# Slot scatters without a bound, slot tiles loaded ahead of features, and squares ahead of products in layer one

## What is computed

```
h = relu(layernorm(x));  x = x + GCN(h)            # two graph convolutions 64 -> 128 -> 64
h = relu(layernorm(x));  x = x + KGAT(h)

def KGAT(h):
    h_proj = einsum('nd,rde->rne', h, relation_weight)      # 32 relations
    att = sum(h_proj[etype, src] * tanh(h_proj[etype, dst] + efeat), -1)
    a = softmax of att over the edges of one destination
    h_nb = segment_sum(h[src] * a, dst)
    return leaky((h + h_nb) @ w1.T) + leaky((h * h_nb) @ w2.T)
```

## Time and profile before

| what | us |
|---|---|
| median of 3 runs | 4033.5 |
| lowest and highest | 4032.55 and 4057.6 |
| the profiled execution, its own time | 4044.76 |
| its span in the profile | 4043.0 |
| busy: POOL / VectorE (DVE) / TensorE (PE) / ScalarE (ACT) | 2830.5 / 2549.4 / 1968.6 / 1865.5 |

### The profile page before, as it was taken

How to read it: one execution, slowest core, us unless ns; L and a number is a source line. 1 busy time by engine, 2 the same in 40 slices (tenths; PEclk the granted TensorE clock), 3 DMA queues, 4 the chain that set the end, 5 groups by cost and what they waited for, 6 DMA issues and landing times.

```text
span 4043.0 us, 42919 instructions
## 1 busy us (share of the span) xinstructions
PE 1968.6 (49%) x10767; PEld 1528.2 (38%) x10767; DVE 2549.4 (63%) x5153; ACT 1865.5 (46%) x5179; POOL 2830.5 (70%) x4049
## 2 busy tenths in 40 slices
PE   5719996576666322222100005524545475766663
PEld 2206664455545312222100004413434454665553
DVE  9957775777777489999732215754866456443442
ACT  0018884667667477778310013102212113887773
POOL 8888884888885488888577776666666400877787
PEclk9959997555555555555555557657656666666666
DMA  6667874444544366666422225325334331221220
GB/s 228 232 252 251 266 261 154 138 154 159 158 141 148 104 196 211 206 207 203 118 61 79 67 82 150 91 58 146 101 97 128 113 89 47 70 58 55 61 61 21
DMA packets 261704, 547.95 MB, mean 136 GB/s; under 512 B 107792, under 2 KB 119930, under 8 KB 261462
## 3 DMA queue, kind: packets, MB, share of 16 engines
q1 hardware_dynamic: 179702, 445.68, 33.0%
q0 software_dynamic: 81760, 99.52, 9.9%
HBM read 275.18 MB, written 273.83 MB: 136 GB/s over the span
## 4 chain that ended last, share of the span: by engine, by line
POOL 38%; issue 16%; ACT 11%; PE 10%; DVE 7%; DMA 3%; POOLq 0%; SPq 0%; DVEq 0%; ACTq 0%
POOL arena L1348 19%; POOL result L1343 9%; POOL slot_rows L1343 8%; ACT work L1519 3%; ACT work L1530 3%; PE banks L1879 2%; DMA work<-slot_rows 2%; PE banks L1846 2%; POOL pause L1356 2%; PE banks L1947 1%; ACT arena L1590 1%; PE banks L2027 1%; ACT work L1753 1%; PE banks L1871 1%; ACT work L1762 1%
## 5 line engine op out<-in xcount | busy, mean ns | idle before, releaser
L1343 POOL DMA_INDIRECT result<-work,outi x392 | 474.8, 1211 | 315.4 <-DVE work L1050 193.8
L1343 POOL DMA_INDIRECT slot_rows<-work,dsafe x392 | 396.5, 1011 | 282.1 <-POOL pause L1361 186.1
L1348 POOL DMA_INDIRECT work<-in_x,dsafe x392 | 439.1, 1120 | 112.6 <-POOL pause L1356 104.9
L1348 POOL DMA_INDIRECT arena<-g_by_node_and_edge,m_idx x392 | 433.5, 1106 | 116.1 <-POOL pause L1356 108.2
L1348 POOL DMA_INDIRECT arena<-h_by_node_and_edge,m_idx x392 | 406.0, 1036 | 111.5 <-POOL pause L1356 59.9
L1348 POOL DMA_INDIRECT arena<-input_and_place_by_node,src_i x252 | 302.6, 1201 | 74.9 <-POOL pause L1356 73.0
L1838 PE MATMUL banks<-ident,work 128*128 128x128 f32 x392 | 101.7, 411 | 462.5 <-ACT arena L1501 410.2
L1933 PE MATMUL banks<-ident,work 128*128 128x128 f32 x556 | 123.6, 366 | 388.5 <-DMA work<-slot_rows 277.4
L1530 ACT ACTIVATE work<-work,q_stat 128x64 f32<-128x64 f32 x784 | 264.7, 428 | 1.0 <-DVE q_stat L624 0.9
L1519 ACT ACTIVATE work<-work,q_stat 128x64 f32<-128x64 f32 x784 | 260.2, 338 | 0.0
L1838 PEld LDWEIGHTS banks<-ident,work 128*128 128x128 f32 x392 | 70.2, 217 | 484.9 <-issue 426.9
(11 more groups left out here) (338 smaller groups left out, 6910.3 us busy)
## 6 DMA issues: line engine op xcount, KB each, us to landing
slot_rows<-work SPq DMA_DIRECT2D x64, 834.0 KB
work<-slot_rows SPq DMA_DIRECT2D x139, 384.0 KB, 3.4
input_and_place_by_node<-arena SPq DMA_DIRECT2D x49, 528.0 KB, 3.0
g_by_node_and_edge<-arena SPq DMA_DIRECT2D x49, 512.0 KB
arena<-x_of_destination SPq DMA_DIRECT2D x56, 448.0 KB, 5.1
work<-g_by_node_and_edge SPq DMA_DIRECT2D x49, 512.0 KB, 3.7
h_by_node_and_edge<-work SPq DMA_DIRECT2D x49, 512.0 KB, 2.7
work<-h_by_node_and_edge SPq DMA_DIRECT2D x56, 448.0 KB, 4.0
```

What stands on the lines that cost most here:

```text
L1343: pool.indirect_dma_start(out=table[:, :], out_offset=bass.IndirectOffsetOnAxis(ap=idx, axis=0), in_=of, in_offset=None, bounds_check=boun ...
L1348: pool.indirect_dma_start(out=to, out_offset=None, in_=table[:, :], in_offset=bass.IndirectOffsetOnAxis(ap=idx, axis=0)).then_inc(signal, 16)
```

## The change

Four edits. (1) The table `slot_rows` gets 392 more rows, `slots_found` lowers each slot number to at most `P*KS + column`, and the slot scatters are issued without a bound, by a new helper; padding rows now land in the extra rows, which nothing reads. (2) SyncE issues the first 3 tile groups of step s inside step s, ahead of `load_features(s + 2)`; before, they came in step s + 1. (3) In the edge stage of layer one ScalarE does `squares(k)` ahead of `turned_and_products(k)`. (4) The views of the table that are read or zeroed are cut to the old rows.

```diff
-        slot_t = nc.dram_tensor("slot_rows", (P * KS, RW), F32).ap()
+        slot_t = nc.dram_tensor("slot_rows", (P * KS + KE, RW), F32).ap()
...
-                os.did(ts(slot_row[:, lo:hi], slot_row[:, lo:hi], float(t0), None, ALU.add))
+                os.do(ts(slot_row[:, lo:hi], slot_row[:, lo:hi], float(t0), None, ALU.add))
+                os.did(stt(out=slot_row[:, lo:hi], in0=tile_no[:, 0:hi - lo], scalar=float(P * KS + lo), in1=slot_row[:, lo:hi],
+                           op0=ALU.add, op1=ALU.min))
...
             for s in range(GE):
-                if s > 0:
-                    load_tiles(s - 1, True)
                 if s + 1 < GE:
                     load_hd(s + 1)
                 if s > 0:
                     load_tiles(s - 1, False)
+                load_tiles(s, True)
                 if s + 2 < GE:
                     load_features(s + 2)
-            for s in (GE - 1, GE):
-                load_tiles(s, True)
-                load_tiles(s, False)
+            load_tiles(GE - 1, False)
+            load_tiles(GE, True)
+            load_tiles(GE, False)
...
+            def scatter_all(table, idx, of, signal):
+                pool.indirect_dma_start(out=table[:, :], out_offset=bass.IndirectOffsetOnAxis(ap=idx, axis=0),
+                                        in_=of, in_offset=None).then_inc(signal, 16)
...
-            def scatter_slowly(table, idx, of, bound, signal):
-                scatter(table, idx, of, bound, signal)
+            def scatter_slowly(table, idx, of, signal):
+                scatter_all(table, idx, of, signal)
...
                 for k in beside_e(g - 1) if g else ():
+                    squares(k)
                     turned_and_products(k)
-                    squares(k)
...
             for k in beside_e(GE - 1):
+                squares(k)
                 turned_and_products(k)
-                squares(k)
```

More of the change, by code:

```diff
@@ L1195, in step_q @@
                         load(node_block(out, b, lo, hi), qout[lo:hi, b % 2], q_out[b % 2])
-            lanes = slot_t.rearrange("(l s) w -> l (s w)", l=P)
+            lanes = slot_t[0:P * KS, :].rearrange("(l s) w -> l (s w)", l=P)
             sp.wait_ge(filled, 7)
@@ L1287, in _ @@
             load(rel_sb[D:P, :, D:P], relations, loaded)
-            slots = slot_t.rearrange("(l s) w -> l s w", l=P)
+            slots = slot_t[0:P * KS, :].rearrange("(l s) w -> l s w", l=P)
             def load_slots(j):
@@ L1426, in send_rows @@
                     t = g * GT + k
-                    (scatter_slowly if s > PART_STEPS[1] else scatter)(slot_t, slot_row[:, t:t + 1], perm[:, q, k, :],
-                                                                       P * KS - 1, c_sent[q])
+                    (scatter_slowly if s > PART_STEPS[1] else scatter_all)(slot_t, slot_row[:, t:t + 1], perm[:, q, k, :],
+                                                                           c_sent[q])
             for s in range(3):
```

## The result

The kernel after the change takes 3908.49 us, the median of four executions (3897.68 to 3921.14), against 4033.4 before: a ratio of 0.9677, 95% interval [0.9631, 0.9724], about 3.2% faster. The prediction was 3887, range 3855 to 3935: the median lies in the range, but 21 us above the forecast and so outside its inner band of 15. The profiled execution of after took 3897.68 us and its span is 3896.0; before it was 4044.76 and 4043.0.

| part of the span, us | gain predicted | gain in the profiles |
|---|---|---|
| up to scatter 0, layer one with it | -0.6 | 20.1 |
| steps 0 to 8, from scatter 0 to scatter 9 | 5 | 2.6 |
| steps 9 to 24, from scatter 9 to scatter 25 | 121.6 | 106.3 |
| the 14 scatters of step 25 | 7.6 | 8.0 |
| from their end to scan 27 | 9.2 | 3.1 |

The account below looks back on a forecast made before the run. POOL's own instruction list was taken to pace slot steps 9 to 25, with VectorE's scores the chain afterwards. Gains of 143.3 + 4 - 0.6 = 147 us from the 4033.5 us median gave 3887 us, range 3855 to 3935.

Parts of the forecast that it names:

- fallen twice: Signs against the forecast: scatter gap stays 0.78 us, POOL waits for L1680 in mid-stage, or layer one ends elsewhere.
- the rival that the gap is the scatter's own: Slot stage: removing the bound does not shorten the scatters' gap, only 9 + 4 us remain, 4020 us; chance 6%.
- The 5 us in steps 0 to 8: Early slot steps: only scatter duration differs, 0.99 against 0.95 us, so 9 x 14 x 0.04 = 5 us gained.
- 39.8 us from scatter to scatter: Slot steps 9 to 25: POOL's step falls to 39.8 us once each scatter loses its long gap.
- first L902 of a full step less than a microsecond behind the scan: Full slot steps: VectorE's first score follows its scan L894 within a microsecond; the wait moves ahead of the fourth.
- the first rival, VectorE as the bound: Slot stage: scores take 3.5 instead of 3.07 us because tile loads land later; 36 us back, 3923 us; chance 13%.
- Its 9 us: Step 25 to scan 27: three scores, 9.2 us, move into VectorE's wait because their tiles are loaded earlier.
- what lets part 1 work: Full slot steps: with late tiles kept, VectorE needs 47.3 us against POOL's 39.8 and would become the bound.
- near 3074: End of the slot stage: VectorE's scan of step 27 ends at 3073.8 instead of 3217.1, a gain of 143.3 us.
- So 0 in each step: Layer one's edge stage: squares first only moves ScalarE's copies and waits, no instruction leaves the chain, gain 0 per step.
- The rival that part 3 gains: Layer one: the squares cover half of ScalarE's waits, 32 us more gained, 3855 us; chance 8%.
- Descriptors on the ports: Slot stage: a denser VectorE would stretch POOL's DMA instructions to 1.21 us, 89 us back, 3976 us; chance 5%.

Follow-up runs that it names:

- a_only: The kernel before with only the bound on the slot scatters removed, loads and squares as before: 3938.48 us, ratio 0.9734.
- turn_first: The changed kernel with ScalarE copying a step's first turned tile group before it waits for VectorE's scan: 3891.01 us, ratio 0.9611.
- b_only: The kernel before with only the load order changed, three tile groups ahead of the features: 4028.43 us, ratio 0.9979.
- after_2: The changed kernel run once more, unaltered, in a second set of runs on one chip: 3907.84 us, ratio 0.9672.

## Why the prediction was right, and where its steps were not

By its own words the forecast should have fallen twice: POOL does wait for the copy behind the scan (L1680, now L1685) in the middle of the stage, and layer one ends 20 us early, L1626 at 1335.80. The number came out in its range all the same, and that is partly luck.

**The bound.** Right in its size and place: a gap of 0.78 us became 0.27 or 0.28, and idle time before the scatters fell by 0.48 us each (0.836 to 75.2 / 209 = 0.360). The sight of it in a_only excludes the rival that the gap is the scatter's own. The 5 us in steps 0 to 8 were read from two single rows; the mean scatter there went from 0.995 to 0.977 us, and 2.6 us came.

**POOL's period.** The step "39.8 us from scatter to scatter" was right of POOL's list (39.6) and 0.9 too small for the stage, 651.1 / 16 = 40.7. This is the step that failed: "first L902 of a full step less than a microsecond behind the scan". The prediction saw that the tiles would be there and forgot that the first score also has ScalarE's two copies before it, and so comes 5.4 us behind the scan in seven of the eight full steps (4.5 in the last). With them the full steps need more than 39.8 and VectorE falls back until POOL stands in steps 15, 20 and 24 to 27. Of the 14.3 us (651.1 - 16 x 39.8) POOL's waits for the copy are 10.7, in steps 15, 20 and 24. So the first rival, VectorE as the bound, held in part, and by another cause than late tiles; turn_first gives 10 to 13 us back.

**Part 2.** Its 9 us were right for a kernel in which VectorE stands idle ahead of scatter 25's end (b_only, 10.3). In after VectorE is late. The picks that come ahead of step 26's scan run on until the last scatter of step 25 has ended (3034.1); then come that scan and two more picks, and the first score starts 10.9 us behind the scatter's end, where it was 11.4 before. So three scores had next to no idle time to move into, and 3.1 us remained of the 9.2. VectorE's timeline, first and last of the earlier picks, L890 of step 26, the first score, and scan 27:

```profile
3011.77 0.46 DVE L941 TENSOR_SCALAR spare<-banks,lane_no 128x256 bf16<-128x256 f32 x1
...
3035.42 0.32 DVE L950 SCALAR_TENSOR_TENSOR spare<-pos,src_i,banks 128x104 f16<-128x104 f16 x1
...
3035.66 1.67 DVE L890 TENSOR_TENSOR work<-work,ends 128x896 f32<-128x896 f32 x1
...
3045.01 0.42 DVE L904 TENSOR_TENSOR dinv_e<-banks,work 128x256 f32<-128x256 f32 x1 [2.55 <-PE banks L1952]
...
3074.87 2.16 DVE L896 TENSOR_TENSOR_SCAN work<-work 128x960 f32<-128x960 f32 x1
```

In exchange part 2 is worth 16 us in the middle of the stage. There the prediction had called it "what lets part 1 work"; a_only shows that part 1 brings 87 of its 106 us without it, since VectorE spends its lead before it holds up POOL. Scan 27 ends at 3077.0, where "near 3074" was forecast: a hit by luck, since the 20 us that layer one gained hide the 23 that the slot stage lacks.

**Part 3.** "So 0 in each step" was wrong by about 20 us. It counted ScalarE's instructions, and rightly said that the waits of the copies would only change place (63.7 us before, 66.5 after). It left out that TensorE's instructions change their length with the granted clock, 1.22 us or 0.69 for the same projection, and the granted clock with what TensorE did just before. The rival that part 3 gains had a chance of 8% and another mechanism, squares over waits of these copies, which the rows exclude.

**Descriptors on the ports.** In steps 9 to 24 VectorE is busier than before, 69% of the time instead of 61%. In the groups of the earlier trace rows and of after a gather took 1.066 us instead of 1.021, a scatter 0.992 instead of 1.025: no stretch like the 1.21 of layer one. The Trainium skill, SBUF — State Buffer, section "SBUF: two separate sides", lets GpSimd's descriptor work wait for VectorE's two-port modes; the 4% on the gathers would be compatible with it, the scatters show nothing of it. In after_2 the gathers between scatter 9 and 25 took 1.040, so half of the 4% is spread.

**The sum.** The slot stage up to scan 27 gave 120.0 us instead of 143.3, and the part ahead of it 20 instead of nothing. Two misses of opposite sign met, by luck, in a sum that was right against the one profiled execution. The medians lie 125 us apart, 22 less than the two profiled executions, of which that of before was above its median and that of after below. Part of that spread is in place: the start of layer one's edge stage alone lies at 671 to 690 us in these profiles.

## What to carry to other kernels

When a wait is taken out of the engine that leads, follow the chain of the next engine through every engine that it passes, to the copies queued ahead on a third: that a transfer is early enough is only its first link. A reorder on one engine with the same instructions is not free or worthless by that: look at what stands right before the matmuls on the path, dense work or an idle wait, and read the granted clock there. And test parts alone before an agreeing sum is believed.

## What had not been expected of the hardware

- An indirect scatter that is given a bound starts 0.78 us behind the pause ahead of it, one without 0.27, as a gather does. It is seen only where each DMA stands behind such a pause and the wait for it: in steps without pauses the gap was 0.30 before with the bound too.
- The same 64x512 projection takes 1.22 or 1.06 us at a granted clock of 0.50 (1.2 GHz) and 0.69 or 0.59 at 1.00 (2.4 GHz). In the 21 groups with a dense run of residual products ahead, it was the wait behind that run that told them apart: 0.7 to 1.6 us in after, 3.6 to 6.0 before. Filler that raised the time at full clock from 7% to 22% shortened no projection where it stood in the wrong place, and cost 31 us.
